# A two-layer sequence kernel: the g tables of the first twelve slots turned by TensorE and kept in DRAM in both forms, one row layout for all slots, fewer and larger DMAs

## The chip, the cores and the metric

The kernel runs on one core of a Trainium2 chip. The metric is the device time of one execution in microseconds (us), the median of repeated runs. The engines are called as in the profile: PE (TensorE), PEld (its weight loads), DVE (VectorE), ACT (ScalarE), POOL (GpSimd) and SP, which here does nothing but issue DMAs and wait; its queue stands in the profile as SPq.

## The reference

Two residual layers over x (64 batches, 128 channels, 2048 steps). The first mixes channels with a matrix chosen by batch; the second convolves each channel along time with its own long kernel, adds a direct term and masks by the batch's length.

```
x = x + einsum('bct,bcd->bdt', x, weights[condition])          # 64 mixes, 128x128 by 128x2048
K = 2*real(einsum('hn,hnl->hl', Ct, exp(dtA*l)))               # 128 kernels of 2048 taps, 64 modes each
y = irfft(rfft(K, 4096) * rfft(x, 4096))[..., :2048] + x*D     # causal convolution by channel
x = x + y * (arange(2048) < length[b])
```

## The kernel before, in words

**Mixing.** For each batch n, x[n] (1 MB) is loaded into an `x_f` buffer, PE multiplies it by `w_buf` (the chosen matrix plus the identity) in four quarters of 512 columns, and ACT and DVE copy the quarters out of PSUM into two halves `stage`. `store_half` (L381 to L387) writes a half to DRAM scratch in two DMAs: channels 0 to 47 to `u_wide`, in pieces of 512 elements (2 KB), channels 48 to 127 to `u_full`, in rows of 1024 (4 KB).

**Slots.** The convolution works by channel, in 64 slots. A wide slot takes four channels and half of the batches, a full slot two channels and all batches. The order is twelve wide slots (0 to 11, first half of the batches, channels 0 to 47), then 40 full slots with the twelve second halves of the wide ones between them, one after every third full slot. For a slot, `load_u` brings the rows back into `u_row`; PE turns them (`transpose_u`, L747), ACT and DVE split them into two f16 parts `u_t`; PE makes the states of the chunks (`inputs_to_state`, L765, with the turned table `gt_sb`), steps them from chunk to chunk (`advance`, L781, seven steps with ACT and DVE between), and makes the outputs from the toeplitz table `toep` (L803, L809) and from the states with the table `g_sb` (L822). ACT scales the outputs out, DVE lays the unmasked input over them (L1226), and SP stores them (L449 for wide, L454 for full slots).

**The tables.** POOL makes `g_sb` for a pair of channels (two pairs in a wide slot). It is needed in two forms: as it is, and turned, as `gt_sb`. The turned one comes from DMA transposes on SP's queue, two for each pair (`transpose_g`, L424 to L439). For the twelve first wide slots the plain form is stored to `g_scratch` too (L439), and the second halves load it back (L419) and transpose it again.

**Three stages.** The first 35 batches (`FIRST = 35`) are mixed alone: stage A. The other 29 are mixed beside slots 0 to 9: stage B (`mixing_slot`); the lists `MIXED` and `QUARTERS` say how many quarters PE does in each of the eight steps k of a slot. In stage B `x_f` has three buffers and `stage` four halves. From slot 10 (`LATER`) on there are slots alone: stage C. All DMAs but seven are issued by SP, in the order in which its code is written; every wait of one holds up all behind it. In slot c, SP works for c - 2 and c - 1 (outputs), c + 1 (tables, last rows) and c + 2 (first rows), and PE turns rows of slot c + 1 between the products of slot c - 1.

Of the kernel before, what the change touches and what calls it, by code (L numbers as in the profile page):

```python
# [8 lines left out]
F32 = mybir.dt.float32  # L9
# [39 lines left out]
QUARTERS = {2: (1, 1, 1, 1, 1, 1, 1, 1), 3: (2, 1, 2, 1, 2, 1, 2, 1)}  # L49
# [29 lines left out]
ST_NO = [sum(SLOTS[r].wide == SLOTS[s].wide for r in range(s)) for s in range(NSL)]  # L79
# [4 lines left out]
MIX_AT = [[[] for _ in range(8)] for _ in range(NSL + 2)]  # L84
for c, number in enumerate(MIXED):
    n0 = FIRST + 1 + sum(MIXED[:c])
    quarters = [(n, k) for n in range(n0, n0 + number) for k in range(4)]
    for k in range(8):
        for _ in range(QUARTERS[number][k]):
            MIX_AT[c][k].append(quarters.pop(0))  # L90

# [12 lines left out]
def u_bank(s, q):  # L104
    return 4 + (q % 2 if s <= LATER else q)
# [18 lines left out]
def build(nc, x, cond, length, w_in, log_dt, c_in, log_a, a_im, d_in, out):  # L124

    u_wide = nc.dram_tensor("u_wide", [H1, 2, P, UNIT], F32, kind="Internal")
    u_full = nc.dram_tensor("u_full", [H - H1, P, HALF], F32, kind="Internal")
    k_dram = nc.dram_tensor("k_scratch", [H, 2, KROW], F16, kind="Internal")
    g_dram = nc.dram_tensor("g_scratch", [H1 // 2, P, 4 * Q], F16, kind="Internal")  # L130

    ctx = ExitStack()
    with ctx:
# [8 lines left out]
        len_i = sb("len_i", [P, 3], I32)  # L142
# [10 lines left out]
        mask = sb("mask", [P, 4 * Q], U8)  # L153
        mask_w = sb("mask_w", [P, 2, UNIT], U8)
# [10 lines left out]
        st_full = [sb(f"st_full{i}", [P, 4 * UNIT], F16, later) for i in range(2)]  # L165
        sb("w_pad", [P, WS * H], F32, later)
        u_row3 = [sb("u_row3", [P, T], F32, later)]
        toep_later = [sb(f"toep{i}", [P, 2, 2, Q], F16, later) for i in range(4, 8)]
        gt_later = [sb(f"gt_sb{i}", [P, 2, 2, 2, P], F16, later) for i in range(2, 4)]
# [28 lines left out]
        st_wide = [sb(f"st_wide{i}", [P, 4 * UNIT], F16, tables) for i in range(2)]  # L198
        g_x = [sb(f"g_x{i}", [P, 2, Q], F32, tables) for i in range(2)]
        g_y = sb("g_y", [P, 2, Q], F32, tables)  # L200
        g_sb = [sb(f"g_sb{i}", [P, 2, 2, Q], F16, tables) for i in range(GS)]
        gt_sb = [sb(f"gt_sb{i}", [P, 2, 2, 2, P], F16, tables) for i in range(2)] + gt_later
        lam_sb = [sb(f"lam_sb{i}", [P, 2, 2, 2, NM], F16, tables) for i in range(LS)]
        toep = [sb(f"toep{i}", [P, 2, 2, Q], F16, tables) for i in range(4)] + toep_later
# [39 lines left out]
        s_row = [[sem(f"s_row{i}_{h}") for h in range(4)] for i in range(4)]  # L244
# [6 lines left out]
        s_gst = [sem(f"s_gst{i}") for i in range(GS)]  # L251
# [28 lines left out]
        def batch_mixed(eng, n):  # L280

            if n < FIRST:
                eng.wait_ge(s_mm, n + 1)
            else:
                eng.wait_ge(s_mq, 4 * (n - FIRST + 1))

        def stage_free(eng, m):
            wait(eng, s_us[STAGE_AT[m]], 32 * uses(STAGE_AT, m))

        def stages_landed(eng, buffers, batches):  # L290

            for b in buffers:
                eng.wait_ge(s_us[b], 32 * STAGE_AT[:2 * batches].count(b))

        def mixing_over(eng):
            eng.wait_ge(s_mq, 4 * (NB - FIRST))

        def width(s):
            return NBW if SLOTS[s].wide else NB

        def groups(s):
            return 2 if SLOTS[s].wide else 4

        def channels(s):
            return 4 if SLOTS[s].wide else 2

        def at(s, j):

            g = groups(s)
            return (j % g * (NJ // g) + j // g) * width(s)  # L310

        def state_tile(s):
            return (st_wide if SLOTS[s].wide else st_full)[ST_NO[s] % 2]

        def st_at(s, h, part):

            w = NJ * width(s)
            return (2 * h + part) * w

        def state(s, part, j):  # L320
            w = NJ * width(s)
            return ap(state_tile(s), part * w + at(s, j), [[2 * w, channels(s)], [1, width(s)]])

        def new_state(s, j):
            return ap(bank, at(s, j - 1), [[NJ * width(s), channels(s)], [1, width(s)]])

        def u_at(s, h, tb, part, g):

            if SLOTS[s].wide:
                return 2 * UNIT * h + UNIT * part + 2 * P * tb + P * g  # L330
            return 2 * UNIT * (2 * h + tb) + UNIT * part + P * g

        def x_at(s, h, tb, g):
            if SLOTS[s].wide:
                return UNIT * h + 2 * P * tb + P * g
            return UNIT * (2 * h + tb) + P * g

        def tab(s, h):

            return TABS[s][h // 2], h % 2  # L340
# [9 lines left out]

        def loads_of_g(t):

            return sum(not SLOTS[SLOT_OF[r]].made for r in range(t % GS, t + 1, GS))

        def quarter_place(n, k):
            return stage[STAGE_AT[2 * n + k // 2]][:, UNIT * (k % 2):UNIT * (k % 2 + 1)]

        def store_last(eng, j, v):

            eng.wait_ge(s_ov, 4 * NSL - 1 + v)  # L360
            dst = bass.AP(out.tensor, (H - 1) * T + j * HALF + v * UNIT, [[H * T, NB], [1, UNIT]])
            eng.dma_start(dst, o_sb[3][j * NB:(j + 1) * NB, v, :]).then_inc(s_store[3], 16)

        @block.sync
        def _(sp):
# [10 lines left out]
            def store_half(n, j):  # L376
                if n < FIRST:
                    sp.wait_ge(s_ev, 2 * n + j + 1)
                else:
                    sp.wait_ge(s_ev, 2 * n + j + 1)  # L380
                    sp.wait_ge(s_evd, 2 * (n - FIRST) + j + 1)  # L381
# [7 lines left out]
            def load_u(s, h):  # L389
                b, last = ROW_AT[s], before(ROW_AT, s)  # L390
                if SLOTS[s].wide:
                    if last is not None:
                        sp.wait_ge(s_ov, 4 * last + h + 1)
                    src = bass.AP(u_wide, ((SLOTS[s].first + h) * 2 + SLOTS[s].part) * (P * UNIT), [[UNIT, P], [1, UNIT]])
                    sp.dma_start(u_row[b][:, UNIT * h:UNIT * (h + 1)], src).then_inc(s_row[b][h], 16)
                else:
                    if last is not None:
                        sp.wait_ge(s_ov, 4 * last + 2 * h + 2)
                    src = bass.AP(u_full, (SLOTS[s].first - H1 + h) * (P * HALF), [[HALF, P], [1, HALF]])
                    sp.dma_start(u_row[b][:, HALF * h:HALF * (h + 1)], src).then_inc(s_row[b][h], 16)  # L400

            def load_toeplitz(s):
                for t in TABS[s]:
                    b, last = TOEP_AT[t], before(TOEP_AT, t)
                    if last is not None:
                        sp.wait_ge(s_out, 4 * (SLOT_OF[last] + 1))
                    src = bass.AP(k_dram, PAIR_OF[t] * (4 * KROW), [[1, P], [KROW, 4], [1, Q]])
                    sp.dma_start(toep[b][:, :, :, :].rearrange("p h a t -> p (h a) t"), src).then_inc(s_t[b], 16)

            def load_g(s):  # L410

                for t in TABS[s]:
                    b = t % GS
                    sp.wait_ge(s_out, 4 * (SLOT_OF[t - GS] + 1))
                    if SLOT_OF[t - GS] < WIDE:
                        sp.wait_ge(s_gst[b], 16 * ((t - GS) // GS + 1))
                    kept = PAIR_OF[t]
                    sp.wait_ge(s_gst[kept % GS], 16 * (kept // GS + 1))
                    sp.dma_start(g_sb[b][:, :, :, :].rearrange("p h a t -> p (h a t)"), g_dram[PAIR_OF[t], :, :])\  # L419
                        .then_inc(s_gl[b], 16)  # L420

            def transpose_g(s):

                for t in TABS[s]:  # L424
# [3 lines left out]
                    sp.sem_inc(s_go, 1)  # L428
                    if SLOTS[s].made:
                        sp.wait_ge(s_g, 4 * (MADE_NO[t] + 1))  # L430
                    else:
                        sp.wait_ge(s_gl[t % GS], 16 * loads_of_g(t))
                    sp.sem_inc(s_go, 1)
                    for lo in (0, NM):
                        sp.dma_start(gt_sb[b][:, :, :, :, lo:lo + NM].rearrange("p h a b m -> p (h a b) m"),  # L435
                                     g_sb[t % GS][NM - lo:P - lo, :, :, :].rearrange("p h a t -> p (h a t)"),
                                     transpose=True).then_inc(s_gt[b], 16)
                    if s < WIDE:
# [845 lines left out]
```

## Time and profile before

| | |
|---|---|
| time, median of 3 runs | 1270.88 us (1268.12 to 1271.56) |
| profiled execution | 1265.78 us |
| its span | 1263.5 us |
| busy in the span: PE, DVE, ACT, POOL | 1054.1, 756.5, 560.3, 623.3 us |
| DMA | 330.91 MB in 238476 packets, 262 GB/s on average |
| DMA transposes among SP's issues | 176 |

A busy PE is not PE at its peak, and its busy time gets longer when the granted clock is low. The page gives one mean over three stages with different limits, so the stages have to be read apart.

### The profile page before, as it was taken

What the parts mean: (1) busy time and instruction counts of PE and PEld (TensorE: products, weight loads), DVE (VectorE), ACT (ScalarE), POOL (GpSimd) and SP (SyncE); (2) the same over time, 40 slices, a digit from 0 to 9 for tenths busy, and PEclk for the clock granted to TensorE, in tenths of its full rate; (3) what the DMA queues carried; (4) which work ended last, traced back from release to release, by engine and by line L of the source; (5) the groups of instructions that cost most, each with busy time, mean ns of one, the idle gap of its engine ahead of it and who ended that gap; (6) DMA issues with size and microseconds to landing.
All of it is one profiled execution on the core that took longest, in us unless ns stands there. A gap on an engine that the chain in (4) does not pass through costs nothing.

```text
span 1263.5 us, 33041 instructions
## 1 busy us (share of the span) xinstructions
PE 1054.1 (83%) x12718; PEld 803.1 (64%) x12718; DVE 756.5 (60%) x1744; ACT 560.3 (44%) x1251; POOL 623.3 (49%) x1396
## 2 busy tenths in 40 slices
PE   8767774777767666785889999999999999999998
PEld 5223342454545444455768888888888878888886
DVE  4989710444334234333567777777777777777775
ACT  3533342333223223323345655655555555555554
POOL 3101427652344442223545757667568558657650
PEclk9988896889878878888999999999999999999999
DMA  9999999999998999998999999999899999999996
GB/s 344 393 340 398 401 353 306 264 307 271 272 264 250 265 246 254 248 245 204 167 209 258 256 210 249 254 227 249 208 272 248 214 260 256 221 249 249 199 243 155
DMA packets 238476, 330.91 MB, mean 262 GB/s; under 512 B 110242, under 2 KB 155682, under 8 KB 230130
## 3 DMA queue, kind: packets, MB, share of 16 engines
q1 hardware_dynamic: 238002, 328.35, 97.9%
q8 instruction: 103, 1.69, 0.6%
q0 software_dynamic: 160, 0.20, 0.2%
q14 instruction: 51, 0.42, 0.1%
q10 hardware_dynamic: 160, 0.26, 0.1%
HBM read 164.96 MB, written 140.71 MB: 242 GB/s over the span
## 4 chain that ended last, share of the span: by engine, by line
PE 53%; DMA 21%; SPq 19%; issue 4%; DVE 2%; ACT 2%; ACTq 0%
PE bank L803 10%; PE bank L822 10%; PE bank L765 8%; DMA u_row<-u_wide 7%; PE bank L747 7%; DMA u_row<-u_full 7%; SPq L435 6%; DMA u_full<-stage 5%; PE bank L781 5%; PE bank L713 5%; PE bank L726 4%; PE bank L809 4%; SPq L385 3%; SPq L387 2%; SPq L449 2%
## 5 line engine op out<-in xcount | busy, mean ns | idle before, releaser
L747 PE MATMUL bank<-ident,u_row 128*128 128x128 f32 x1024 | 287.0, 284 | 138.9 <-DMA u_row<-u_wide 120.2
L803 PE MATMUL bank<-toep,u_t 128*128 128x192 f16 (+1 forms) x3072 | 351.2, 223 | 0.3 <-issue 0.3
L603 POOL TENSOR_TENSOR g_sb<-g_x,g_sb 128x128 f16<-128x128 f32 x256 | 115.3, 484 | 348.5 <-ACT g_sb L891 348.5
L747 PEld LDWEIGHTS bank<-ident,u_row 128*128 128x128 f32 x1024 | 147.1, 145 | 158.9 <-DMA u_row<-u_wide 108.5
L803 PEld LDWEIGHTS bank<-toep,u_t 128*128 128x128 f16 x3072 | 237.0, 100 | 15.3 <-issue 3.9
L1204 DVE SCALAR_TENSOR_TENSOR u_t<-bank,u_t 128x512 f16<-128x512 f32 x256 | 176.3, 689 | 111.1 <-ACT u_t L920 110.0
L809 PE MATMUL bank<-toep,x_t 128*128 128x64 f16 x2048 | 193.2, 195 | 2.0 <-issue 2.0
L822 PE MATMUL bank<-g_sb,st_full 128*128 128x256 f16 x960 | 192.4, 274 | 0.2 <-issue 0.2
L920 ACT ACTIVATE u_t<-bank 128x512 f16<-128x512 f32 x256 | 151.6, 593 | 72.9 <-PE bank L747 72.3
L713 PE MATMUL bank<-x_f,w_buf 128*128 128x512 f32 x280 | 138.0, 644 | 45.6 <-issue 30.7
L765 PE MATMUL bank<-u_t,gt_sb 128*128 128x224 f16 (+1 forms) x1056 | 157.4, 302 | 9.0 <-issue 9.0
L809 PEld LDWEIGHTS bank<-toep,x_t 128*128 128x128 f16 x2048 | 161.6, 100 | 2.6 <-issue 2.2
L935 ACT ACTIVATE st_full<-bank 128x128 f16<-128x128 f32 x280 | 77.5, 277 | 174.4 <-PE bank L781 133.2
L942 ACT ACTIVATE o_sb<-bank 128x512 f32<-128x512 f32 x256 | 152.8, 597 | 4.0 <-PE bank L822 4.0
L619 POOL TENSOR_TENSOR w_buf<-w_f,ident 128x128 f32<-128x128 f32 x64 | 34.3, 538 | 222.9 <-PE bank L713 116.2
L765 PEld LDWEIGHTS bank<-u_t,gt_sb 128*128 128x128 f16 x1056 | 102.2, 98 | 54.8 <-issue 17.1
L713 PEld LDWEIGHTS bank<-x_f,w_buf 128*128 128x128 f32 x280 | 55.3, 205 | 123.1 <-issue 104.9
L726 PE MATMUL bank<-x_f,w_buf 128*128 128x512 f32 x232 | 130.9, 676 | 0.0
L1226 DVE COPY_PREDICATED o_sb<-mask,u_row 128x512 f32<-128x512 uint8 x160 | 123.5, 772 | 11.4 <-issue 11.3
L595 POOL TENSOR_TENSOR g_x<-g_x,g_y 128x128 f32<-128x128 f32 x256 | 127.3, 529 | 5.0
L610 POOL TENSOR_TENSOR lam_sb<-eyes,lam_v 128x128 f16<-128x128 f16 x256 | 118.9, 495 | 19.3 <-PE bank L781 19.3
L1209 DVE TENSOR_TENSOR st_full<-bank,st_full 128x128 f16<-128x128 f32 x280 | 81.7, 292 | 74.3 <-ACT st_full L935 71.2
(138 smaller groups left out, 1519.7 us busy)
## 6 DMA issues: line engine op xcount, KB each, us to landing
x_f<-in_x SPq DMA_DIRECT2D x64, 1024.0 KB, 10.5
out<-o_sb SPq DMA_DIRECT2D x254, 256.0 KB
u_full<-stage SPq DMA_DIRECT2D x128, 320.0 KB, 8.9
u_row<-u_full SPq DMA_DIRECT2D x80, 512.0 KB, 6.3
u_wide<-stage SPq DMA_DIRECT2D x128, 192.0 KB, 6.4
u_row<-u_wide SPq DMA_DIRECT2D x96, 256.0 KB, 8.7
toep<-k_scratch SPq DMA_DIRECT2D x88, 256.0 KB, 7.0
g_scratch<-g_sb SPq DMA_DIRECT2D x24, 256.0 KB, 4.5
```

Of the source, the lines that this page charges most:

```text
L595: pool.tensor_tensor(out=g_x[r][:, h, part], in0=g_x[r][:, h, part], in1=g_y[:, h, part], op=SUB)\
L713: last = pe.matmul(bank[:, 4 * (n % 2) + k, :], w_buf[n % WS][:, :], x_f[X_AT[n]][:, k * 512:(k + 1) * 512], start=True, stop=True)
L726: pe.matmul(bank[:, 6 + k % 2, :], w_buf[n % WS][:, :], x_f[X_AT[n]][:, k * 512:(k + 1) * 512], start=True, stop=True).then_inc(s_mq, 1)
L747: ins = pe.transpose(bank[:, u_bank(s, q), k % 4 * P:(k % 4 + 1) * P], ap(u_row[b], (h * groups(s) + g) * Q + tb * P, [[1, P]]), ident[:, :])
L765: last = pe.matmul(to, gt_sb[GT_AT[t]][:, hh, a, 1 - tb, :], ap(u_t[s % 3], u_at(s, h, tb, b, 0), [[1, cols]]), start=(m == 0 and fresh), ...
L803: pe.matmul(bank[:, y, col + tb * P + NM:col + Q], ap(u_t[s % 3], u_at(s, h, tb, a, gr), [[1, P]]), tp[:, hh, b, NM:Q - tb * P], start=fir ...
L809: pe.matmul(bank[:, y, col + tb * P:col + tb * P + NM], ap(x_t[s % 2], x_at(s, h, tb, gr), [[1, P]]), tp[:, hh, b, 0:NM], start=False, sto ...
L822: last = pe.matmul(bank[:, y, col:col + Q], ap(state_tile(s), st_at(s, h, a) + gr * P, [[1, P]]), g_sb[t % GS][:, hh, b, :], start=False, ...
L920: act.activation(u_t[s % 3][:, q, 0, :], bank[:, u_bank(s, q), :], ACT.Copy, scale=US).then_inc(s_uh, 1)
L942: act.activation(o_sb[o][:, v % 2, :], bank[:, 2 + v % 2, :], ACT.Copy, scale=1.0 / (US * KS))\
L1204: dve.scalar_tensor_tensor(out=t[:, q, 1, :], in0=bank[:, u_bank(s, q), :], scalar=US, in1=t[:, q, 0, :], op0=MUL, op1=SUB).then_inc(s_ul, 1)
L1226: dve.copy_predicated(o_sb[2 * (s % 2) + v // 2][:, v % 2, :].rearrange("p (b t) -> p b t", t=P), where.rearrange("p (b t) -> p b t", t=P) ...
```

## The change

1. **Turning g.** For slots 0 to 11 the table is turned by PE: four matmuls for each channel against `swap`, a permutation matrix, into PSUM bank 6 or 7, which ACT or DVE copies to `gt_sb`. These turns and the quarters of the mixing are now one list of units, `UNITS`; a turn of slot c + 1 comes in each of steps 4 to 7 of slot c, and the two banks alternate from unit to unit. The DMA transposes stay for the 40 full slots.
2. **Both forms kept.** `store_g` writes a wide slot's two pairs in one DMA of 512 KB to `g_scratch` and another to the new `gt_scratch`. The second halves of the wide slots load both forms; before, they loaded one and transposed it. A turn may overwrite `gt_sb` only when its store has landed (`stored_g`).
3. **One row layout.** `u_scratch` holds every channel in pieces of 512 elements (2 KB) by half of the batches. A staged half is stored in one DMA (two before), a slot's rows are loaded in two DMAs of 512 KB (a wide slot had four of 256 KB), and a full slot works on four views, channel by half of the batches, as a wide one does. Full slots' outputs are stored in four DMAs with 2 KB rows (before, four with 4 KB rows, two at a time). There is one set of state tiles, `st_sb`.
4. **Toeplitz tables** of two neighbouring pairs are loaded in one DMA where their buffers lie side by side.
5. **Order.** Batches up to 35 use all six `x_f` buffers (before, up to 31). `QUARTERS` of a slot with three batches is (2, 2, 2, 2, 1, 1, 1, 1), before (2, 1, 2, 1, 2, 1, 2, 1). SP loads the first half of slot c + 2's rows at step 5, the second at step 0 of the next slot.

```diff
-QUARTERS = {2: (1, 1, 1, 1, 1, 1, 1, 1), 3: (2, 1, 2, 1, 2, 1, 2, 1)}
+QUARTERS = {2: (1, 1, 1, 1, 1, 1, 1, 1), 3: (2, 2, 2, 2, 1, 1, 1, 1)}
-X_AT = [n % XS if n < NBW else n % (XS // 2) for n in range(NB)]
+X_AT = [n % XS if n <= FIRST else n % (XS // 2) for n in range(NB)]
...
-                dst = bass.AP(u_wide, ((n // NBW * 4 + 2 * j) * NBW + n % NBW) * UNIT,
-                              [[2 * P * UNIT, H1], [NBW * UNIT, 2], [1, UNIT]])
-                sp.dma_start(dst, stage[b][0:H1, :].rearrange("p (a t) -> p a t", t=UNIT)).then_inc(s_us[b], 16)
-                dst = bass.AP(u_full, (j * NB + n) * HALF, [[P * HALF, H - H1], [1, HALF]])
-                sp.dma_start(dst, stage[b][H1:H, :]).then_inc(s_us[b], 16)
+                dst = bass.AP(u_dram, (n // NBW * P + 2 * j * NBW + n % NBW) * UNIT, [[2 * TILE, H], [NBW * UNIT, 2], [1, UNIT]])
+                sp.dma_start(dst, stage[b][:, :].rearrange("p (a t) -> p a t", t=UNIT)).then_inc(s_us[b], 16)
...
+            def store_g(s):
+                t = TABS[s][0]
+                r = t // 2 % (GS // 2)
+                sp.wait_ge(s_g, 4 * (MADE_NO[t] + 2))
+                dst = bass.AP(g_dram, PAIR_OF[t] * P * 4 * Q, [[4 * Q, P], [P * 4 * Q, 2], [1, 4 * Q]])
+                sp.dma_start(dst, ap(g_all, t % GS * 4 * Q, [[4 * Q, 2], [1, 4 * Q]])).then_inc(s_gst[r], 16)
+                for unit in turns_of(s):
+                    evacuated(sp, UNIT_OF[unit])
+                dst = bass.AP(gt_dram, PAIR_OF[t] * P * 4 * Q, [[4 * Q, P], [P * 4 * Q, 2], [1, 4 * Q]])
+                sp.dma_start(dst, ap(gt_now, 0, [[4 * Q, 2], [1, 4 * Q]])).then_inc(s_gtst[r], 16)
...
+        def unit_copy(eng, u):
+            unit, half = UNITS[u], bank[:, 6 + u % 2, :]
+            eng.wait_ge(s_mq, u + 1)
...
+            s, last = SLOT_OF[unit.of], before(GT_AT, unit.of)
+            if last is not None:
+                eng.wait_ge(s_st, 7 * SLOT_OF[last] + 1)
+                stored_g(eng, last)
...
+                    pe.wait_ge(s_g, 4 * (MADE_NO[of] + 1))
+                    evacuated(pe, u - 2)
+                    for k in range(4):
+                        last = pe.matmul(to[:, k * P:(k + 1) * P], g_sb[of % GS][:, part, k // 2, k % 2 * P:(k % 2 + 1) * P],
+                                         swap[:, :, :].rearrange("p a m -> p (a m)"), start=True, stop=True)
...
             def mixing_slot(c):
...
-                    if k == 3:
-                        if c == 0:
-                            sp.wait_ge(s_kd, 80)
-                            load_toeplitz(c)
-                        transpose_g(c + 1)
-                    if k in (3, 5, 7):
-                        if has(c - 1):
-                            store_out(c - 1, k // 2 - 1)
-                        load_u(c + 2, k // 2 - 1)
+                    if k == 1:
+                        store_g(c)
+                    if k in (3, 5, 7) and has(c - 1):
+                        store_out(sp, c - 1, k // 2 - 1)
+                    if k == 5:
+                        load_u(c + 2, 0)
```

**SP in stage B.** These are SP's rows of the kernel before for the first half of the work that it does in slot 2, from the loading of the toeplitz tables (L408) over the last rows of slot 3 (L395) to the transposes (L435) and the stores of g (L439).

```order
L408 DMA toep<-k_scratch 128x4x256 x2
L449 DMA out<-o_sb 4x32x512
L395 DMA u_row<-u_wide 128x512
L385 DMA u_wide<-stage 48x2x512
L387 DMA u_full<-stage 80x1024
L385 DMA u_wide<-stage 48x2x512
L387 DMA u_full<-stage 80x1024
L374 DMA x_f<-in_x 128x2048
L435 DMA_TRANSPOSE gt_sb<-g_sb 128x8x64 x2
L439 DMA g_scratch<-g_sb 128x1024
L435 DMA_TRANSPOSE gt_sb<-g_sb 128x8x64 x2
L439 DMA g_scratch<-g_sb 128x1024
```

The same place of the changed kernel, where L440 is the toeplitz load, L395 an output store, L426 the load of rows, L417 the store of a staged half, L448 and L452 the stores of both forms of g, and L407 the load of x:

```order
L440 DMA toep<-k_scratch 128x8x256
L395 DMA out<-o_sb 4x32x512
L426 DMA u_row<-u_scratch 128x2x512
L417 DMA u_scratch<-stage 128x2x512
L448 DMA g_scratch<-g_sb 128x2x1024
L452 DMA gt_scratch<-gt_sb 128x2x1024
L417 DMA u_scratch<-stage 128x2x512
L407 DMA x_f<-in_x 128x2048
L417 DMA u_scratch<-stage 128x2x512
L395 DMA out<-o_sb 4x32x512
```

The transposes are gone, each store of a half is one row, and the stores of g stand behind the slot's first store of a mixed half. Over a whole slot with three batches, 31 DMAs are now 18.

**PE in stage B.** The kernel before, in slot 0, from the products that make the states (L765) on; L747 turns rows, L726 is a quarter of the mixing, L781 a step of the states.

```order
L765 MATMUL bank<-u_t,gt_sb 128x224 x24
L747 MATMUL bank<-ident,u_row 128x128 x2
L726 MATMUL bank<-x_f,w_buf 128x512 x2
L781 MATMUL bank<-st_wide,lam_sb 128x32 x12
L747 MATMUL bank<-ident,u_row 128x128 x2
L726 MATMUL bank<-x_f,w_buf 128x512
L781 MATMUL bank<-st_wide,lam_sb 128x32 x12
L747 MATMUL bank<-ident,u_row 128x128 x2
L726 MATMUL bank<-x_f,w_buf 128x512 x2
L781 MATMUL bank<-st_wide,lam_sb 128x32 x12
```

The same place of the changed kernel; L797, L774, L752 and L814 are those four, and L758 is a turn of g.

```order
L797 MATMUL bank<-u_t,gt_sb 128x224 x24
L774 MATMUL bank<-ident,u_row 128x128 x2
L752 MATMUL bank<-x_f,w_buf 128x512 x2
L814 MATMUL bank<-st_sb,lam_sb 128x32 x12
L774 MATMUL bank<-ident,u_row 128x128 x2
L752 MATMUL bank<-x_f,w_buf 128x512 x2
L814 MATMUL bank<-st_sb,lam_sb 128x32 x12
L774 MATMUL bank<-ident,u_row 128x128 x2
L752 MATMUL bank<-x_f,w_buf 128x512
L758 MATMUL bank<-swap,g_sb 128x128 x4
L814 MATMUL bank<-st_sb,lam_sb 128x32 x12
```

More quarters stand in the first steps of the slot, and from step 4 on each step has four more matmuls, a turn for slot 1.

## Rows read from the trace of the kernel before

**Rows 1.** The windows, stretches that end where slots 0, 10 and 15 begin

```profile
core 0: us, PE busy (x) PEld busy (x) DVE busy (x) ACT busy (x) POOL busy (x), PEclk, DMA share, GB/s
0.00:180.00 180.00, 142.64 (x566) 66.22 (x566) 127.40 (x315) 73.43 (x76) 36.71 (x100) 0.94 0.99 376
180.00:229.00 49.00, 21.02 (x53) 10.36 (x52) 6.36 (x12) 12.47 (x18) 33.40 (x81) 0.69 1.02 303
229.00:577.00 348.00, 249.56 (x2303) 168.15 (x2302) 133.57 (x278) 105.83 (x241) 136.82 (x348) 0.85 0.96 260
577.00:662.00 85.00, 64.80 (x943) 55.54 (x941) 48.40 (x110) 36.28 (x90) 35.67 (x81) 0.96 0.96 192
662.00:1244.00 582.00, 561.20 (x8635) 490.95 (x8634) 431.40 (x1005) 325.89 (x812) 380.68 (x788) 1.00 1.02 239
```

**Rows 2.** Waits of PE, then of SP, in 229 to 577 us (us, times, longest)

```profile
PE bank L747 <- DMA u_row<-u_wide: 95.7, 25, 8.1
...
SPq L381 <- DVE stage L1191: 5.5, 2, 3.9
...
SPq L408 <- PE bank L822: 0.4, 1, 0.4
```

**Rows 3.** Timeline of SP from 486 us: issues (start, duration)

```profile
486.54 5.13 SPq L435 DMA_TRANSPOSE gt_sb<-g_sb  x2
...
492.71 3.04 SPq L435 DMA_TRANSPOSE gt_sb<-g_sb  x2
```

**Rows 4.** Lines of SP, 220 to 590 us: duration of an issue, ns min/median/max

```profile
L435 SPq DMA_TRANSPOSE gt_sb<-g_sb x40: 1209/1760/3822, 237.3 to 563.5; - x40
L385 SPq DMA_DIRECT2D u_wide<-stage x58: 302/786/2347, 223.2 to 578.5; - x58
```

**Rows 5.** DMA view: traffic of 40 to 180 us, then of 229 to 577 us

```profile
DMA packets 15253, 53.32 MB, mean 381 GB/s; under 512 B 2780, under 2 KB 2780, under 8 KB 12161
...
DMA packets 60175, 90.43 MB, mean 260 GB/s; under 512 B 25296, under 2 KB 35536, under 8 KB 56844
```

**Rows 6.** DMA view, 620 to 1240 us: KB each, median us to landing

```profile
u_row<-u_full SPq DMA_DIRECT2D x75, 512.0 KB, 6.2
u_row<-u_wide SPq DMA_DIRECT2D x48, 256.0 KB, 8.2
```

**Rows 7.** Groups of PE, 229 to 577 us; chain at 481 us; ACT from the page

```profile
L726 PE MATMUL bank<-x_f,w_buf 128*128 128x512 f32 x220 | 123.4, 671 | 0.0
L822 PE MATMUL bank<-g_sb,st_wide 128*128 128x256 f16 x222 | 52.9, 310 | 0.0
...
481.42 0.11 PE bank L747
482.33 1.72 PE bank L726 x4
...
L920 ACT ACTIVATE u_t<-bank 128x512 f16<-128x512 f32 x256 | 151.6, 593 | 72.9 <-PE bank L747 72.3
```

**Rows 8.** Waits of PE in 180 to 229 us, then SP's transposes for slot 0

```profile
PE bank L747 <- DMA u_row<-u_wide: 17.2, 1, 17.2
PE bank L713 <- DMA x_f<-in_x: 9.8, 1, 9.8
...
189.72 6.95 SPq L435 DMA_TRANSPOSE gt_sb<-g_sb  x2
197.48 6.69 SPq L435 DMA_TRANSPOSE gt_sb<-g_sb  x2
```

**Rows 9.** Waits of PE in 577 to 662 us

```profile
PE bank L747 <- DMA u_row<-u_full: 9.5, 6, 2.2
PE bank L747 <- DMA u_row<-u_wide: 7.4, 4, 2.9
```

**Rows 10.** Waits of SP in 662 to 1244 us

```profile
SPq L433 <- DMA g_sb<-g_scratch: 25.4, 11, 3.0
```

**Rows 11.** Tile u_full, all its DMAs over the whole span

```profile
DMA to landing us min/median/max: 3.5/7.5/14.1
```

More of the change, by code:

```diff
@@ L324, in new_state @@
[L324 to L340, printed above, removed]
+            batch_mixed(eng, NB - 1)
@@ new lines, in load_toeplitz @@
+            def load_toeplitz(s):
+                t0, n = TABS[s][0], len(TABS[s])
+                together = n == 2 and TOEP_AT[t0] % 4 < 3 and TOEP_AT[t0 + 1] == TOEP_AT[t0] + 1
+                for t in [t0] if together else TABS[s]:
+                    for r in range(t, t + 1 + together):
+                        last = before(TOEP_AT, r)
+                        if last is not None:
+                            sp.wait_ge(s_out, 4 * (SLOT_OF[last] + 1))
+                    b, rows_ = TOEP_AT[t], 4 * (1 + together)
+                    src = bass.AP(k_dram, PAIR_OF[t] * (4 * KROW), [[1, P], [KROW, rows_], [1, Q]])
+                    to = ap((toep_now, toep_later)[b // 4], b % 4 * 4 * Q, [[Q, rows_], [1, Q]])
+                    sp.dma_start(to, src).then_inc(s_t[b], 16)
@@ L427, in transpose_g @@
                         sp.wait_ge(s_st, 7 * SLOT_OF[last] + 1)
[L428 to L437, printed above, removed]
@@ new lines, in load_gt, with transpose_g @@
+                    sp.dma_start(gt_sb[b].rearrange("p h a b m -> p (h a b m)"), gt_dram[PAIR_OF[t], :, :]).then_inc(s_gt[b], 16)
+            def transpose_g(s):
+                t = TABS[s][0]
+                b, last = GT_AT[t], before(GT_AT, t)
+                if last is not None:
+                    sp.wait_ge(s_st, 7 * SLOT_OF[last] + 1)
+                    if SLOT_OF[last] < WIDE:
+                        stored_g(sp, last)
+                sp.sem_inc(s_go, 1)
+                sp.wait_ge(s_g, 4 * (MADE_NO[t] + 1))
+                sp.sem_inc(s_go, 1)
+                for lo in (0, NM):
+                    sp.dma_start(gt_sb[b][:, :, :, :, lo:lo + NM].rearrange("p h a b m -> p (h a b) m"),
+                                 g_sb[t % GS][NM - lo:P - lo, :, :, :].rearrange("p h a t -> p (h a t)"),
+                                 transpose=True).then_inc(s_gt[b], 16)
@@ L729, in transpose_u, with unit @@
[L729 to L739 removed]
+            def unit(u):
+                of, part = UNITS[u].of, UNITS[u].part
+                to = bank[:, 6 + u % 2, :]
+                if UNITS[u].batch:
+                    if part == 0:
+                        x_loaded(of)
+                    evacuated(pe, u - 2)
+                    last = pe.matmul(to, w_buf[of % WS][:, :], x_f[X_AT[of]][:, part * 512:(part + 1) * 512],
+                                     start=True, stop=True)
+                else:
+                    pe.wait_ge(s_g, 4 * (MADE_NO[of] + 1))
+                    evacuated(pe, u - 2)
+                    for k in range(4):
+                        last = pe.matmul(to[:, k * P:(k + 1) * P], g_sb[of % GS][:, part, k // 2, k % 2 * P:(k % 2 + 1) * P],
+                                         swap[:, :, :].rearrange("p a m -> p (a m)"), start=True, stop=True)
+                last.then_inc(s_mq, 1)
@@ L925, in fold_toeplitz @@
                     b = TOEP_AT[t]
-                    act.wait_ge(s_t[b], 16 * (uses(TOEP_AT, t) + 1))
+                    if landed_with(t) == t:
+                        act.wait_ge(s_t[b], 16 * (sum(landed_with(r) == r and TOEP_AT[r] == b for r in range(t)) + 1))
                     act.activation(toep[b][0:NM, :, :, 0:NM].rearrange("p h a t -> p (h a) t"),
```

442 lines of the change are left out of this document (215 added, 227 removed).

## The prediction

> **What bounds the kernel now.** The page's totals give no answer: PE is busy for 83% of the span, but the DMA engines are busy nearly all of the time as well. So I read the windows first, cut at the starts of slots 0, 10 and 15 [rows 1]. The reader is to see four different stretches. Until 180 us the DMA engines are 99% busy and move 376 GB/s: stage A is bound by bytes. From 229 to 577 us (ten slots, 34.8 us each) the DMA share is hardly lower, 0.96, but only 260 GB/s are moved, and PE is busy for 249.6 of 348 us at a clock of 0.85. From 662 us on PE is busy for 561.2 of 582 us at full clock: stage C is bound by PE, 47 slots of 12.4 us. Between them lie two handovers, 180 to 229 us, where PE works for 21 of 49 us, and 577 to 662 us, where it works for 65 of 85.
>
> Second, the waits in stage B [rows 2]. PE stands for 95.7 us, nearly all of its idle time, and always for the rows of a wide slot. SP, which issues those loads, waits in turn for almost nobody: its five rows sum to 14.3 us in 348. It is busy with its own issues. Third, the timeline of SP shows on what [rows 3]: the two pairs of transposes of one slot hold it for 5.13 and 3.04 us, and the load of the next slot's rows stands behind them. The median transposing issue takes 1.76 us, that of a store of a half 0.79, though the fastest such store takes 0.30 [rows 4]: so part of SP's time is the ring pushing back, and a DMA saved is not always its whole issue saved.
>
> **Stage B, what goes.** Forty transposes at 1.76 us are 70 us of SP. Four DMAs for the stored halves of a batch become two, four loads of rows become two, two of toeplitz become one: with the transposes 31 DMAs a slot become 18. At the median of 0.79 us the other nine saved would be another 7 us a slot, at the fastest 0.30 us 3 us a slot. SP's load of 34 us a slot falls by 7 for the transposes and by 3 to 7 for the rest, to 20 to 24 us. So SP is no longer the bound, and the 95.7 us of PE's waits can go as far as two other limits let them.
>
> **Stage B, limit of the bytes.** It moves 90.43 MB [rows 5]. The transposes leave with 40 times 0.131 MB, ten stores of turned tables of 0.524 MB come: 90.4 MB again. At the 381 GB/s that the DMAs of 40 to 180 us reach without a transpose beside them [rows 5], that is 237 us; at 310, between the rates of the two stages, 292 us.
>
> **Stage B, limit of PE.** The turns are 16 matmuls of 128 columns a slot. None stands in the trace before. A row transpose of as many columns takes 0.11 us in the chain, the mean of a 256-column matmul is 0.310 us [rows 7]: 1.8 to 5 us a slot, of which I take 1.8, because the chain counts what lies on PE and the mean counts overlaps twice. With them PE has 249.6 + 18 = 268 us at the present clock. That clock is low: a quarter of the mixing takes 0.671 us in the mean and 0.43 where the clock is full (four in 1.72 us) [rows 7], and 220 of them would give 53 us back, 215 us in all. The copies out of PSUM are two a slot for ACT (0.593 us, the nearest row [rows 7]) and two for DVE, about 1.2 us beside 106 and 134 us of work in 348: hidden; were ACT full they would cost 12 us over the stage.
> I take PE's 268 us at the present clock and 4 us of waits left, 272 us: **76 us less**. The bounds are 237 us (111 less) and 292 us (56 less).
>
> The new waits: ACT and DVE, in step 4, may copy a turn only when the stores of step 1 have landed. Behind them stand the steps of the states, for which PE waits. Three steps are about 10 us of a slot of 27; the longest landing of a stored half is 14.1 us [rows 11], so it may cost some us in some slots. SP's load of the first rows of slot c + 2 stands at step 5, with 3 steps, about 9 us, to the use; a 512 KB load took 6.2 us in stage C [rows 6]. I count both within the 4 us and the upper bound.
>
> **Handover from A to B.** The transposes for slot 0 hold SP for 6.95 and 6.69 us, and PE waits for an x for 9.8 us and then for rows for 17.2 [rows 8]. The transposes go, and six x buffers up to batch 35 let x come earlier. But the 49 us carried 303 GB/s, 14.8 MB; at 381 GB/s these need 39 us. I take **10 us less**; the ends are 0 and all 27.
> In stage A itself the bytes are the same and bind. Issues saved there are worth nothing, as the DMA engines are what hides them; 2 KB pieces in place of 4 KB for 80 of 128 channels could cost. Those are 0.31 of the stage's bytes; at the handover's rate of 303 in place of 376 GB/s they would cost 180 x 0.31 x 0.24 = 13 us. In stage A 3/8 of every store has 2 KB pieces already and the engines move 376, so I take 0.
>
> **Handover from B to C.** PE waits 16.9 us for rows [rows 9]. SP still has to see the last stages landed, but no transposes for slot 11. I take half, **8 us less**, ends 0 and 17.
>
> **Stage C.** PE's work is the same, matmul for matmul: the four views of a full slot are taken two at a time where a weight is shared. What can be gained is the 20.8 us that PE is idle. SP waits 25.4 us for the reloaded g before it can transpose it [rows 10]; this wait goes, and four transposes of each of these twelve slots become two loads. Transposes for the 40 full slots stay. I take **12 us less**, ends 0 and 21 less.
>
> **Sum.** 10 + 76 + 8 + 12 = 106 us off the profiled execution's 1265.8 us gives 1160. The median of the runs shown is 5.1 us above that execution, so the forecast is 1165 us.
>
> **Rivals.**
> *Smaller gain.* SP's issues are long because the ring pushes back; with fewer DMAs of the same bytes each takes longer, and the turns' wait for landed stores takes the transposes' place. For it: 0.79 against 0.30 us, and a DMA share of 0.96 in stage B. Against it: 260 GB/s beside 381. Stage B at 300 to 325 us, the rest at half: 23 to 48 off stage B and 15 elsewhere, 1205 to 1235 us.
> *Larger gain.* Once PE stands less, its clock rises to that of the stretches behind it (0.96 and 1.00 [rows 1]), and stage B falls to the bytes' 237 us, with up to 35 us elsewhere: 1105 to 1130 us.
> *Transposes were not the matter.* The DMA engines are 96% busy before, and if a transpose costs them only its bytes, 0.131 MB, they have as many bytes to move as before, and PE waits for the same rows: about 1270 us. Against it stands the difference in rate between the stages, and nothing but transposes, toeplitz tables and outputs is new in B.
> The Trainium skill speaks for this one: "Advanced Engine Details and Errata", section "X-Bar Transpose (TRN2)", has a transposing DMA as fast as a plain one. By that rule, at its 350 to 400 GB/s, an estimate is 0.4 us for the 0.131 MB of each, and the swap for a store would gain nothing. The trace's issues of 1.76 us and the drop in rate do not agree with it.
> *Slower: 2 KB rows everywhere.* In stage C loads of 256 KB in 2 KB rows land in 8.2 us, loads of 512 KB in 4 KB rows in 6.2 [rows 6]. All loads and outputs of the 40 full slots now have 2 KB rows. If that, and not the four transposes beside the wide slots, makes them late, each full slot's loads come later by 2 us and more, and the DMA share of 1.02 in stage C leaves no room. The 106 us gained elsewhere less the 12 of stage C are eaten when each of 47 slots loses 2 us; at 3 us the time is 1177 + 141 = 1318 us. Against it: a load has nearly a slot of lead, and stage A moves most bytes per us with such pieces among its stores.
>
> **How the numbers follow.** Chances: forecast (1130 to 1200 us) 0.65, smaller gain 0.15, larger gain 0.12, transposes no matter 0.03, slower 0.05. Leaving out no more than 2 in 10, the range goes from 1118, inside the larger gain, to 1212 us, inside the smaller. Faster by over 0.3%, which is about what a measurement of this kernel can tell, 0.92; within it 0.03; slower 0.05.
>
> **What would show it.** Right: stage B near 27 us a slot, over 320 GB/s in it, PE's wait for rows down from 95.7 to under 15 us, SP now waiting for others; the first handover near 39 us; stage C near 12.1 us a slot. Wrong: issues of stores of 1.5 us and more in stage B (ring), ACT or DVE waiting for the stores of g, loads of full slots that land after 8 us and PE waiting for them in stage C, or matmuls of the turns near 0.3 us each on the chain.

## The result

The changed kernel is slower: 1380.6 us against 1271.2 us, the ratio 1.086 with a 95% interval of 1.082 to 1.090. The profiled execution has a span of 1381.8 us. The forecast was 1165 us.

The first view is again the windows, cut where slots 0, 10, 15 and 62 begin (the start of L797, the products that make a slot's states; at 212, 514.5, 600 and 1332 us).

```profile
core 0: us, PE busy (x) PEld busy (x) DVE busy (x) ACT busy (x) POOL busy (x), PEclk, DMA share, GB/s
0.00:212.00 212.00, 160.99 (x635) 75.00 (x636) 132.67 (x315) 87.61 (x98) 69.10 (x172) 0.94 1.00 389
212.00:514.50 302.50, 240.99 (x2461) 168.20 (x2460) 144.20 (x297) 116.78 (x260) 132.66 (x333) 0.88 0.87 301
514.50:600.00 85.50, 68.05 (x954) 59.08 (x953) 46.41 (x109) 35.71 (x89) 39.97 (x94) 0.90 0.77 190
600.00:1332.00 732.00, 601.90 (x8472) 511.40 (x8471) 422.94 (x987) 323.50 (x800) 338.33 (x781) 0.93 0.89 185
```

Beside [rows 1]: slot 0 starts 17 us earlier, stage B takes 302.5 us for 348, so at slot 15 the changed kernel is 62 us ahead. Then it loses everything. The same 47 slots took 571 us before (662 to 1233 us) and take 732 us now, 15.6 us each in place of 12.1. PE, once busy nearly all the time, stands for 130 us of 732. Its matmuls are as many as before (8472 and 8471), but they keep it busy for 601.9 us in place of 550.2, at a granted clock of 0.93 in place of 1.00: of the 161 us more, 109 are idle time and 52 are longer work. No resource looks full: the DMA engines are busy for 0.89 (1.02 before) and move 185 GB/s (239 before). A lower rate *and* a lower share, while PE waits for transfers, is what the reader should stop at.

PE's waits in stage C, with SP's, are these.

```profile
PE bank L774 <- DMA u_row<-u_scratch: 106.1, 52, 5.2
```

```profile
SPq L426 <- DVE o_sb L1255: 71.0, 58, 2.2
SPq L395 <- DVE o_sb L1255: 55.3, 51, 2.5
```

The loads of rows are late. In the DMA view of 662 to 1244 us such a load needs 9.6 us from issue to landing ([rows 6] has 6.2 for the same 512 KB), and SP's issues got longer too: a transposing one takes 2.97 us at the median in 600 to 1332 us, 1.42 us before in 662 to 1233 us.

```profile
u_row<-u_scratch SPq DMA_DIRECT2D x75, 512.0 KB, 9.6
```

SP's own line of the transposes:

```profile
L486 SPq DMA_TRANSPOSE gt_sb<-g_sb x36: 1987/2970/7567, 602.9 to 1303.8; - x36
```

What do the engines do while such a load is under way? The DMA view of 996.5 to 1000.5 us, in a full slot, in 40 slices of 0.1 us, answers that; the first row is the busy share of the 16 engines in tenths, the second what they moved.

```profile
DMA  2222222222222222222222323232323232223382
GB/s 102 102 102 102 102 102 102 102 102 102 102 102 102 102 102 102 102 102 102 102 102 82 123 82 123 82 123 82 123 82 123 82 123 82 74 69 97 77 64 28
...
out<-o_sb SPq DMA_DIRECT2D x2, 256.0 KB
u_row<-u_scratch SPq DMA_DIRECT2D x1, 512.0 KB, 10.8
```

I read a flat 102 GB/s at a quarter of the busy share as four of the sixteen engines at work, 25.5 GB/s each, and twelve idle. The DMAs that SP issues there are two output stores and a load of rows that takes 10.8 us. But the flat rate is there before the first of them, so what moves then is older: most likely two output stores that SP had issued one behind the other, nine microseconds earlier, with the load of rows behind them.

```profile
987.75 2.27 SPq L395 DMA_DIRECT2D out<-o_sb  x2
```

Had these two stores run on different engines, they could have gone side by side at twice the rate. The chain of the same slot runs from the overlay of an output into such a load, and PE starts when it has landed:

```profile
989.38 0.67 DVE o_sb L1255
990.04 0.02 issue
990.07 10.71 DMA u_row<-u_scratch
1000.78 0.04 issue
1000.83 0.33 PE bank L774
```

So the theory: **a store on four engines.** Before, a full slot's output went out in DMAs of 64 rows of 4 KB (L454); the changed kernel uses the wide slots' form, whose destination is 4 groups by 32 rows, the outermost dimension 4. By the theory such a DMA is carried by four engines, and always by the same four (the trace doesn't name the engines). They then carry 1.05 MB / 4 = 262 KB of each slot's output, and a sixteenth of the rest (1.05 MB of rows, 0.26 MB of toeplitz, 0.26 MB transposed), 98 KB: 360 KB at 25.5 GB/s are 14.1 us at least, beside 15.6 measured. The same sum for the changed kernel's stage B, 91.07 MB of which 9.4 MB are outputs, is (81.7 / 16 + 9.4 / 4) MB / 25.5 GB/s = 292 us, beside 302.5 measured. The sums are floors, so they allow the theory but do not prove it. The rivals are the forecast's own, 2 KB rows, and SP's queue, busy with longer issues.

The Trainium skill has a rule that says this, in "DMA: Bandwidth & Descriptors", section "Why a DMA increments its semaphore by 16 and not by 1": a DMA is split over the largest number up to 16 that divides the sizes of the outermost dimensions on both sides, and over the lowest-numbered engines. By that rule, 64 rows give 16 engines and 4 by 32 rows give 4; the trace agrees with the four, by its 102 GB/s, and no run here shows which engines they are.

### The profile page after: what moved, and what is told of

Read it like the earlier page. It is cut to its first block, busy times and chain, and to the rows that moved or that the text cites. A ratio compares the mean times of both kernels' runs of the same rounds, so it can differ in the third digit from the quotient of the medians.

```text
span 1381.8 us, 33160 instructions
## 1 busy us (share of the span) xinstructions
PE 1099.5 (80%) x12910; PEld 835.4 (60%) x12910; DVE 763.9 (55%) x1754; ACT 576.3 (42%) x1275; POOL 580.1 (42%) x1377
## 4 chain that ended last, share of the span: by engine, by line
DMA 48%; PE 34%; SPq 7%; DVE 4%; ACT 3%; issue 3%; POOLq 0%; DVEq 0%; POOL 0%; ACTq 0%
DMA u_row<-u_scratch 36%; DMA u_scratch<-stage 9%; PE bank L835 6%; PE bank L853 6%; PE bank L752 6%; PE bank L774 5%; PE bank L797 4%; SPq L395 3%; PE bank L740 3%; PE bank L841 2%; PE bank L814 2%; SPq L462 2%; DVE o_sb L1255 2%; DVE u_t L1233 1%; ACT u_t L949 1%
## 5 line engine op out<-in xcount | busy, mean ns | idle before, releaser
L774 PE MATMUL bank<-ident,u_row 128*128 128x128 f32 x1024 | 295.6, 292 | 188.4 <-DMA u_row<-u_scratch 183.2
L853 PE MATMUL bank<-g_sb,st_sb 128*128 128x256 f16 x1536 | 330.0, 288 | 2.1 <-issue 2.1
L774 PEld LDWEIGHTS bank<-ident,u_row 128*128 128x128 f32 x1024 | 150.5, 148 | 214.5 <-DMA u_row<-u_scratch 195.5
L965 ACT ACTIVATE st_sb<-bank 128x128 f16<-128x128 f32 x448 | 123.9, 277 | 309.3 <-PE bank L814 214.4
L1238 DVE TENSOR_TENSOR st_sb<-bank,st_sb 128x128 f16<-128x128 f32 x448 | 130.2, 291 | 171.2 <-ACT st_sb L965 165.5
L835 PE MATMUL bank<-toep,u_t 128*128 128x192 f16 (+1 forms) x1752 | 208.4, 226 | 0.0
L1255 DVE COPY_PREDICATED o_sb<-mask,u_row 128x512 f32<-128x512 uint8 x256 | 194.5, 760 | 17.0 <-issue 16.9
L853 PEld LDWEIGHTS bank<-g_sb,st_sb 128*128 128x128 f16 x1536 | 156.9, 103 | 11.0 <-issue 2.4
L835 PE MATMUL bank<-toep_later,u_t 128*128 128x192 f16 (+1 forms) x1320 | 156.7, 227 | 2.7 <-issue 2.7
L814 PE MATMUL bank<-st_sb,lam_sb 128*128 128x32 f16 (+1 forms) x3168 | 147.2, 184 | 10.1 <-issue 7.4
L814 PEld LDWEIGHTS bank<-st_sb,lam_sb 128*128 128x128 f16 x3168 | 132.3, 97 | 37.0 <-issue 21.8
L835 PEld LDWEIGHTS bank<-toep,u_t 128*128 128x128 f16 x1752 | 139.7, 103 | 11.0 <-issue 3.5
L752 PE MATMUL bank<-x_f,w_buf 128*128 128x512 f32 x232 | 125.0, 648 | 2.3 <-ACT stage L926 1.9
## 6 DMA issues: line engine op xcount, KB each, us to landing
x_f<-in_x SPq DMA_DIRECT2D x64, 1024.0 KB, 14.1
```

The lines of the kernel that those rows point to most:

```text
L752: last = pe.matmul(to, w_buf[of % WS][:, :], x_f[X_AT[of]][:, part * 512:(part + 1) * 512], start=True, stop=True)
L774: ins = pe.transpose(bank[:, u_bank(s, v), k % 4 * P:(k % 4 + 1) * P], ap(u_row[b], v * UNIT + g * Q + tb * P, [[1, P]]), ident[:, :])
L814: last = pe.matmul(ap(bank, v * 2 * P + at(j), [[2 * P, n], [1, NBW]]), lam_sb[t % LS][:, h, a, :, :].rearrange("p k m -> p (k m)"), st_sb ...
L835: pe.matmul(bank[:, y, col + tb * P + NM:col + Q], ap(u_t[s % 3], v * 2 * UNIT + a * UNIT + tb * 2 * P + gr * P, [[1, P]]), tp[:, h, b, NM ...
L853: last = pe.matmul(bank[:, y, col:col + Q], st_sb[s % 2][:, v, a, gr * P:(gr + 1) * P], g_sb[t % GS][:, h, b, :], start=False, stop=(m == ...
L1238: dve.tensor_tensor(out=state(s, 1, j), in0=new_state(j), in1=state(s, 0, j), op=SUB).then_inc(s_stl, 1)
```

## The experiments

All ratios are to the kernel before on the same chip.

**1. The changed kernel with its outputs on all engines (a_pair).** Two views are stored at once, in four DMAs of 32 rows by 2 views.

```diff
-            eng.wait_ge(s_ov, 4 * s + v + 1)
-            dst = bass.AP(out.tensor, batches(s, v) * NBW * H * T + channel(s, v) * T, [[UNIT, 4], [H * T, NBW], [1, UNIT]])
-            eng.dma_start(dst, o_sb[o][:, v % 2, :]).then_inc(s_store[o], 16)
+            if v % 2 == 0:
+                return
+            eng.wait_ge(s_ov, 4 * s + v + 1)
+            at0, at1 = (batches(s, r) * NBW * H * T + channel(s, r) * T for r in (v - 1, v))
+            for j in range(4):
+                dst = bass.AP(out.tensor, at0 + j * UNIT, [[H * T, NBW], [at1 - at0, 2], [1, UNIT]])
+                eng.dma_start(dst, o_sb[o][NBW * j:NBW * (j + 1), :, :]).then_inc(s_store[o], 16)
...
```

> The changed kernel, with the outputs stored in another cut: for two views at once, one DMA for each quarter of the partitions, 32 rows of 2 KB by two views, in place of one DMA of 4 groups by 32 rows for each view. The bytes, the 2 KB rows and everything else stay; eight DMAs of 128 KB a slot replace four of 256 KB. Then this cut, outermost 32, brings stage C from 15.4 to 11.5 to 12.5 us a slot, stage B from 29 to about 27, and the time to 1150 to 1200 us. Rival (2 KB rows, the one forecast): small rows make loads and stores late; they are all still there, so the time stays within 2% of 1380 us. Rival (SP's queue): SP was busy for 96% of stage C; with four more DMAs a slot it is busier, and the time goes up to 1400 us or more.

Measured: 1125.3 us, ratio 0.886 (0.883 to 0.889), better than the range given. The windows, cut at its slots 0, 10, 15 and 62:

```profile
212.00:467.00 255.00, 234.54 (x2462) 163.68 (x2461) 146.34 (x297) 117.14 (x261) 138.50 (x324) 0.95 0.99 355
467.00:536.00 69.00, 61.09 (x954) 54.66 (x952) 46.63 (x109) 35.42 (x89) 41.64 (x87) 0.95 0.88 257
536.00:1092.00 556.00, 546.45 (x8472) 481.14 (x8471) 423.72 (x988) 321.26 (x800) 383.44 (x796) 1.00 0.97 245
```

Stage C is bound by PE again, 11.8 us a slot, with PE busy for 546 of 556 us. In that stretch a load of rows lands after 5.6 us and a transposing issue takes 1.27 us:

```profile
u_row<-u_scratch SPq DMA_DIRECT2D x93, 512.0 KB, 5.6
```

```profile
L490 SPq DMA_TRANSPOSE gt_later<-g_sb x38: 1193/1272/2657, 546.1 to 1091.3; - x38
```

The 2 KB rows are all still there, and SP has four DMAs more a slot. Both rivals fall. SP's long issues were a result of the stores' shape, not the cause: a transposing one went from 2.97 to 1.27 us while SP got more to do. That the four busy engines kept SP's ring full is the likely way; no run separates it.

**2. The kernel before with the same fault (b_four).** One line of the full slots' store:

```diff
-                        dst = bass.AP(out.tensor, (SLOTS[s].first + v // 2) * T + j * HALF, [[H * T, NB], [1, HALF]])
+                        dst = bass.AP(out.tensor, (SLOTS[s].first + v // 2) * T + j * HALF, [[H * T, 4], [4 * H * T, NB // 4], [1, HALF]])
```

> The kernel before, with each of the two output DMAs of a full slot's channel written with an outermost dimension of 4 (every fourth batch, then 16 rows of 4 KB); the batches land in another order in the output, bytes, row size and number of DMAs are those of before. Theory (four engines): the 40 full slots slow down as in the changed kernel, from 12.1 to about 15 us; 1271 + 40 x 3 = 1390 us, 1350 to 1420. Rivals (2 KB rows, or the order of SP's work): nothing of theirs is changed, 1271 us.

Measured: 1497.0 us, ratio 1.177 (1.173 to 1.182). The sign is the theory's, the size beyond its range. In 700 to 1400 us a load of a full slot's rows landed after 10.5 us (6.2 before):

```profile
u_row<-u_full SPq DMA_DIRECT2D x61, 512.0 KB, 10.5
```

**3. 2 KB rows alone (b_2k).** `[[H * T, NB], [HALF, 2], [1, UNIT]]` in the same place.

> The kernel before, with the outputs of full slots stored in rows of 2 KB in place of 4 KB (the second and third quarter of the time steps are exchanged in the output), outermost dimension 64 as before. Theory (four engines): no change, within 1% of 1271 us. Rival (2 KB rows): half of the rows that the change made small are small here, so half of its 165 us of stage C, 1350 us.

Measured: 1278.1 us, ratio 1.006 (1.002 to 1.010). Small rows in the outputs cost at most 1%. The forecast's reason for a slower kernel was not the true one.

**4. The wide slots' outputs of the kernel before on all engines (b_wide).** The cut of experiment 1, for L449 alone.

> The kernel before, with the outputs of wide slots alone stored in the cut of 32 rows by two views (eight DMAs of 128 KB a slot for four of 256 KB); full slots as they are. The wide slots of before had the outermost dimension 4 already. Theory (four engines): in stage B the four engines carry 784 KB a slot, 32 us at 24.4 bytes per ns, near the 34.8 us found, so relief there is worth something if SP leaves room: 1230 to 1265 us. If SP's issues alone bound stage B, four more of them a slot cost 2 us a slot, 1290 us.

Measured: 1174.5 us, ratio 0.924 (0.921 to 0.928), a gain beyond the range. The kernel before had the fault already, in its 24 wide slots. Its stage B falls from 348 to 295.5 us, and in 662 to 1140 us a load of a wide slot's rows lands after 4.0 us:

```profile
229.00:524.50 295.50, 240.33 (x2302) 161.18 (x2301) 133.75 (x278) 105.22 (x240) 139.71 (x343) 0.89 1.05 305
...
u_row<-u_wide SPq DMA_DIRECT2D x38, 256.0 KB, 4.0
```

The stretch from slot 10 to 15 takes 68 us for 85, and the 47 slots from there on 549 us for 571. That is with every DMA transpose still in place.

**5. Eight engines (b_eight).** `[[H * T, 8], [8 * H * T, NB // 8], [1, HALF]]` in the place of experiment 2.

> The kernel before with the output DMAs of full slots written with an outermost dimension of 8 (every eighth batch, then 8 rows of 4 KB); batches in another order in the output, everything else as before; the partner of b_four (1497 us). Theory (the outermost dimension sets how many engines carry a store, always the same ones): eight engines carry 128 KB of a slot's output each in place of 64, some 5 us of their time against 10 with four; a full slot stays mostly under TensorE's 11.4 us, 1271 to 1320 us. Rival (any extra dimension in the store costs, whatever its size): about 1497 us like b_four.

Measured: 1375.5 us, ratio 1.085 (1.078 to 1.092). The order is right, 16, 8 and 4 engines giving 1271, 1376 and 1497 us, but my range was missed. The sum of bytes by engine gives 0.13 MB of output and 0.1 MB of the rest for each of the eight, 9 us, under the 11.4 us that a full slot takes where PE bounds it (616.0 to 627.4 us in b_wide); the 47 slots from slot 15 on take 14.4 us each here (661.3 to 1337.4 us). So the sum of bytes is a floor, not the price, when engines are loaded unevenly.

**6. and 7. Distance, or dimension?** Experiments 2 and 5 also moved the rows that one engine writes 4 and 8 MB apart. b_near has 4 groups of 15 rows, 1 MB apart as before, and leaves out four of the 64 batches; b_far has 16 groups of 4 rows, 16 MB apart.

```diff
+++ b_near
+                        dst = bass.AP(out.tensor, (SLOTS[s].first + v // 2) * T + j * HALF, [[16 * H * T, 4], [H * T, 15], [1, HALF]])
+++ b_far
+                        dst = bass.AP(out.tensor, (SLOTS[s].first + v // 2) * T + j * HALF, [[H * T, 16], [16 * H * T, NB // 16], [1, HALF]])
```

> The kernel before with the output DMAs of full slots written as 4 groups of 15 rows of 4 KB (the last batch of each group of 16 is left out, 6% of their bytes); rows of one group lie 1 MB apart, as before, and not 4 MB as in b_four. It tells whether the price of b_four comes from the outermost dimension of 4 or from the distance of the rows that one engine writes. Theory (four engines): nearly the price of b_four, less 6% of the bytes, 1440 to 1500 us. Rival (distance): 1271 us, or the part of the price that isn't the distance's.

> The kernel before with the output DMAs of full slots written as 16 groups of 4 rows of 4 KB, the rows of one group 16 MB apart; batches in another order in the output, all bytes there. It is the control of b_four and b_eight: an extra dimension and long distances, but an outermost dimension of 16. Theory (four engines): within 1.5% of 1271 us. Rival (an extra dimension or the distance costs): 1350 us or more.

Measured: b_near 1450.4 us, ratio 1.143 (1.135 to 1.152); b_far 1262.8 us, ratio 0.992 (0.988 to 0.996), both in the theory's ranges. An outermost dimension of 4 costs with near rows, one of 16 costs nothing with far ones. The dimension is the cause.

**8. Full slots alone mended (a_full).** The changed kernel with experiment 1's cut for full slots; wide slots keep the outermost dimension 4.

> The changed kernel with the outputs of the 40 full slots alone stored in the cut of a_pair (32 rows by two views); the wide slots' outputs stay with the outermost dimension 4, as before and in the change. It splits the 255 us between the changed kernel and a_pair. Theory (four engines, and in the full slots it is new): stage C comes back to about 11.9 us a slot but for the twelve wide slots in it, which had this store before too; stage B stays at the changed kernel's 30.3 us a slot, 46 us more than a_pair in all. 1170 to 1215 us. Rival (something else in the full slots' new layout costs as well): well over 1215 us.

Measured: 1191.3 us, ratio 0.935 (0.929 to 0.940), within the range. Of the 255 us between the changed kernel and a_pair, 189 are the full slots', where the change brought the fault in, and 66 the wide slots', where it had been before. Stage B takes 306 us, as in the changed kernel.

**9. The parts of the change that help.** Each starts from a_pair (1125.3 us) and takes one part back. a_dmat turns all tables by DMA again and keeps only the plain form of g, by the old `transpose_g`:

```diff
-UNITS = turns_of(0) + quarters(FIRST)
+UNITS = quarters(FIRST)
...
-                if c + 1 >= WIDE and has(c + 1):
-                    if SLOTS[c + 1].made:
-                        transpose_g(c + 1)
-                    else:
-                        load_gt(c + 1)
+                if has(c + 1):
+                    transpose_g(c + 1)
```

> The kernel a_pair (outputs on all engines) with the tables turned as before: DMA transposes for all slots, no turns by TensorE, only the plain form of g kept and transposed again for the second halves. Row layout, fewer and larger DMAs, order and x buffers are those of the changed kernel. Theory (SP and its transposes were a large part of stage B, as the prediction said): ten slots with four transposes cost back 3 to 5 us each and the first handover 10, so 1165 to 1185 us beside 1125. Rival (the rest of the change, its fewer DMAs and its order, made the gain): within 10 us of 1125.

Measured: 1153.2 us (ratio 0.908, 0.906 to 0.910), 28 us more, under the range, which had 10 us for the first handover where 3 came. Its slot 0 starts at 215 us and its stage B takes 291 us for 255, with 58.1 us of PE's waits for rows for 18.3, so the turns by PE and the freed queue are worth 36 us there, 3.6 a slot; some is made up later.

a_order takes back the order of the quarters and the x buffers, with two loads of x that go with them:

```diff
-QUARTERS = {2: (1, 1, 1, 1, 1, 1, 1, 1), 3: (2, 2, 2, 2, 1, 1, 1, 1)}
+QUARTERS = {2: (1, 1, 1, 1, 1, 1, 1, 1), 3: (2, 1, 2, 1, 2, 1, 2, 1)}
-X_AT = [n % XS if n <= FIRST else n % (XS // 2) for n in range(NB)]
+X_AT = [n % XS if n < NBW else n % (XS // 2) for n in range(NB)]
...
+            load_x(FIRST + 2)
...
+            load_x(FIRST + 3)
```

> The kernel a_pair with the old order of the quarters (2, 1, 2, 1, 2, 1, 2, 1) and the old x buffers (six up to batch 31, three from 32 on), everything else kept. If the earlier x loads made the first handover shorter, it is 5 to 10 us slower; if the order of the mixing gives nothing of its own, stage B stays at 25.5 us a slot. 1125 to 1140 us.

Measured: 1138.3 us (ratio 0.894, 0.891 to 0.897), 13 us more, within the range but not for its reason: slot 0 starts at 209 us, no later than in a_pair, and stage B takes 273 us for 255. The two edits weren't separated.

a_split stores every staged half in two DMAs again, `for h0, h1 in ((0, H1), (H1, H))`.

> The kernel a_pair with every store of a staged half in two DMAs again (channels 0 to 47, 48 to 127), both in 2 KB rows: 128 DMAs more, same bytes. If SP's issues still limit stage B, six more a slot at 0.4 to 0.8 us cost 2 to 5 us a slot, 1145 to 1175 us. If the bytes bind, nothing, within 1% of 1125 us.

Measured: 1160.5 us (ratio 0.913, 0.911 to 0.915), within the range, 35 us more for 128 DMAs: 23 in stage B (278 us) and 12 before it. The parts overlap, since their 28, 13 and 35 us sum to more than the 49 us between b_wide and a_pair.

## Why the prediction was wrong

**Stage C is the step that failed.** The forecast said that PE's work is the same and that only its 20.8 idle us could change, 12 us less. It became 161 us more: the idle time went to 130 us, 106 of them waits for rows, and the same matmuls took 52 us more at the lower clock. For the DMAs I had weighed bytes, rows and numbers of issues, and taken the sixteen engines for one pool, in "stage A moves most bytes per us with such pieces among its stores" as well. The shape of the output store went from 64 rows to 4 groups by 32 rows, and it was the outermost 4 that counted. The trace before had a sign of it: in [rows 6] 256 KB of a wide slot's rows land later than 512 KB of a full slot's. I put that to the transposes or the row size; in b_wide, whose loads are the same and whose transposes are all there, they land after 4.0 us, so it was mostly the wide outputs on four engines. I had even listed the outputs among the three things that are new in stage B, and looked at the transposes alone. (The 12.4 us a slot was a slip: 662 to 1244 us holds more than 47 slots, which take 12.1 each.)

**The rival on the slower side had the place and the sign, but the wrong mechanism.** Loads of full slots did land after more than 8 us, and PE did wait for them, as it had said. But 2 KB rows cost at most 1% in the outputs (b_2k), and a_pair keeps them all.

**Stage B: right direction, too large, with the wrong bound.** 76 us were forecast, 45 came. PE was busy for 241 us, less than the 268 taken; the term that was too small is its waits, 4 us in the sum and 59.6 measured:

```profile
PE bank L774 <- DMA u_row<-u_scratch: 59.6, 11, 9.0
```

SP is no longer the bound, as said: it waits for others for 110 us of the stage (14.3 before), and a store of a half takes it 0.39 us, so the sign of the ring did not come. What took its place was not in the forecast: neither the ring, nor the bytes of all engines, but the four engines that carry the wide outputs, 292 us by the sum above. With that bound gone (a_pair) the stage takes 255 us, 93 less, between my 76 and my best case of 111; the clock rises from 0.85 to 0.95, as the rival of the larger gain had it. That rival's range was not what its terms give: 111 and 35 us off 1271 are 1125 us, and nothing in it leads down to 1105. That a_pair measured 1125.3 us is luck, since it has other outputs and, in stage B, other terms.

**What a DMA transpose was worth.** I had put 70 us on SP's 40 transposing issues. Taking them back costs 36 us in stage B (a_dmat), and b_wide gains 52 us in that stage with all of them in place. So my reading of "SP is busy with its own issues" was half of the story. It held: in b_wide SP still waits for others for only 9.8 us of its stage B. But PE's waits for rows fell there from 95.7 to 50.9 us by the outputs alone, and part of the length of an issue wasn't the transpose's own: the median transposing issue in stage B is 1.76 us before, 1.58 in b_wide and 1.27 in a_dmat.

**The turns by PE** were sized well. All 192 are 19.5 us of PE's time, 1.6 a slot for the twelve slots, 1.8 were taken:

```profile
L758 PE MATMUL bank<-swap,g_sb 128*128 128x128 f16 x192 | 19.5, 230 | 9.4 <-ACT stage L936 8.9 <-ACT gt_sb L926 0.5
```

Nor did the copies wait for the stores of g, but for once on ACT and once, for 1.3 us, on DVE:

```profile
ACT gt_sb L926 <- DMA gt_scratch<-gt_sb: 7.3, 1, 7.3
```

**Handovers and stage A.** Slot 0 starts 17 us earlier, 10 were forecast. Part of it comes from stage A itself, where I had said that issues saved are worth nothing: in 40 to 180 us the changed kernel moves 414 GB/s against 381 [rows 5], and a_split, with two stores a half, 387.

```profile
DMA packets 19512, 57.98 MB, mean 414 GB/s; under 512 B 1852, under 2 KB 1852, under 8 KB 15968
```

From slot 10 to 15 nothing was gained of the 8 us forecast, and 16 us once the outputs use all engines.

**What stays open.** Why b_four costs more than the changed kernel with the same four engines, and b_eight much more than its bytes; that DMAs behind a slow one are held back in rings that are full is likely, since issues and landings both get longer, but no run separated it. Open too is why the two stores of a half in a_split cost time in stage A, whose stores have 48, 80 or 128 rows and by the theory use all 16 engines.

The best version found is a_pair, 1125.3 us, 11.4% under the kernel before.

## What to carry to other kernels

Read the shape of each DMA's outermost dimension on both sides, not its bytes alone: where a change gives a store or a load an outermost 4 in place of 64, a few engines carry it all, and what is issued behind it comes late (here loads of rows after 9.6 us in place of 5.6). When PE waits for transfers while the rate falls, look at the DMA row in slices of 0.1 us: a flat fraction, such as a quarter of the busy share at 102 GB/s, is a sign. Its absence clears nothing: in b_four, with the same four engines by the theory, the mean share over the same 47 slots (668.7 to 1452.8 us) is 1.01, about that of before, and only the rate tells, 174 GB/s in place of 240. And a queue with long DMA issues need not be the cause: here a transposing issue fell from 2.97 to 1.27 us when the outputs' shape alone changed, so look at the shapes of the stores before removing issues.

## What the runs showed that was not expected

Four DMAs of 128 KB on all engines are far better than two of 256 KB on four: 255 us of 1381 in this kernel. One store of 512 KB for a half batch in place of one of 192 and one of 320 KB, with the same bytes, raised the rate of stage A, with its DMA share at 1.00, from 387 to 414 GB/s.
